# Four mixing layers on one image, the scan layer: TensorE's products grouped by array form, the state contribution moved behind y by channel into its own columns

## The reference, cut to what matters

```python
dA_cs = jnp.cumsum(dA, axis=2)                                   # within the chunk
Lmat = jnp.exp(dA_cs[:, :, :, None, :] - dA_cs[:, :, None, :, :])
att = einsum('bcihn,bcjhn->bcijh', Ch, Bh) * Lmat * dtc          # causal part only
y_intra = einsum('bcijh,bcjhp->bcihp', att, xc)
states = einsum('bcjhn,bcjh,bcjhp->bchpn', Bh, decay_to_end * dtc, xc)
new = carry * dec + st                                           # from chunk to chunk
y_inter = einsum('bcihn,bcih,bchpn->bcihp', Ch, exp(dA_cs), prev_states)
y = y_intra + y_inter + D * x                                    # then LayerNorm over 384, * norm_w + norm_b
out = (y * z) @ out_proj_w.T                                     # z from the input by a projection
```

## Time and profile before

| | before |
|---|---|
| median of three runs | 2561.39 us |
| the profiled execution | 2555.05 us, span of its instructions 2553.0 us |
| mean granted TensorE clock | 0.956 |
| TensorE products, weight loads | busy 2232.7 us (87%), 1652.4 us (65%) |
| VectorE, ScalarE, GpSimd | busy 1667.8, 1305.3, 1113.0 us |
| the scan's steady turns | from about 949 to 1877 us of the span |

### The profile page before, as it was taken

The page is one execution under the profiler, slowest core; times in us unless marked ns, Lnnn a source line. Parts: engine busy times, 40 slices in busy tenths (PEclk is TensorE's granted clock), DMA queues, the critical chain, the costliest instruction groups (busy, mean ns, idle before and its releaser), DMA issues. The chain is left out here.

```text
span 2553.0 us, 63276 instructions
## 1 busy us (share of the span) xinstructions
PE 2232.7 (87%) x22485; PEld 1652.4 (65%) x22612; DVE 1667.8 (65%) x3120; ACT 1305.3 (51%) x2719; POOL 1113.0 (44%) x1393
## 2 busy tenths in 40 slices
PE   0699997998999169999999999999968999789998
PEld 0575645786788047777777777777756656366563
DVE  5345585674575168888888888888863455734557
ACT  0245540084057147777777777777733454334543
POOL 0333150000000147878787878778743222432225
PEclk9999997999999579999999999999989999989999
DMA  8623395415523312222222222222235045950349
GB/s 207 176 78 69 85 330 155 119 31 208 171 41 122 112 42 60 59 59 59 58 60 56 61 56 62 55 61 57 59 87 157 2 89 153 310 165 15 79 123 317
DMA packets 305576, 272.33 MB, mean 107 GB/s; under 512 B 175534, under 2 KB 238798, under 8 KB 299162
## 3 DMA queue, kind: packets, MB, share of 16 engines
q1 hardware_dynamic: 294650, 256.15, 36.1%
q0 software_dynamic: 9280, 6.44, 2.1%
q10 hardware_dynamic: 1496, 7.63, 0.8%
HBM read 165.44 MB, written 81.46 MB: 97 GB/s over the span
## 5 line engine op out<-in xcount | busy, mean ns | idle before, releaser
L1664 DVE TENSOR_TENSOR l_scan_att<-l_scan_decay,l_scan_causal_scores 128x512 f32<-128x512 f32 x384 | 327.4, 853 | 64.2 <-ACT l_scan_decay L1633 64.0
L714 ACT COPY l_arena<-l_body_bank 128x384 f32<-128x384 f32 x192 | 141.3, 897 | 308.3 <-PE l_body_bank L591 308.3
L1627 ACT ACTIVATE l_scan_decay<-l_scan_cum 128x512 f32<-128x512 f32 x384 | 216.3, 597 | 34.4 <-PE l_scan_cum L1519 34.3
L1633 ACT ACTIVATE l_scan_decay<-l_scan_decay 128x512 f32<-128x512 f32 x384 | 227.8, 631 | 4.1
L810 DVE TENSOR_TENSOR l_freq<-l_body_bank,l_filter 128x512 f32<-128x512 f32 x144 | 99.6, 692 | 183.8 <-PE l_body_bank L604 183.8
L1644 ACT ACTIVATE l_scan_yw<-l_scan_y_by_channel,l_scan_norm_b,l_scan_norm_w 128x128 f32<-128x128 f32 x384 | 148.0, 456 | 127.8 <-PE l_scan_y_by_channel L1581 126.8
L1566 PE MATMUL l_scan_gate_projected<-l_scan_xr,l_wf 97*128 97x128 f32 (+1 forms) x1536 | 206.6, 284 | 1.3 <-DVE l_scan_xo L1719 1.2
L1597 PE MATMUL l_scan_gate_projected<-l_scan_yz,l_scan_wo 128*96 128x128 f32 x1536 | 198.5, 279 | 1.1 <-DVE l_scan_yz L1696 1.1
L1597 PEld LDWEIGHTS l_scan_gate_projected<-l_scan_yz,l_scan_wo 128*96 128x96 f32 x1536 | 170.9, 163 | 40.0 <-issue 29.6
L571 POOL TENSOR_TENSOR l_arena<-l_arena 96x512 f32<-96x512 f32 x96 | 122.7, 1278 | 167.2 <-ACT l_arena L779 162.5
L1484 POOL TENSOR_TENSOR l_scan_inter<-l_scan_inter,l_scan_xd 128x384 f32<-128x384 f32 x128 | 128.0, 1000 | 152.5 <-DVE l_scan_inter L1679 152.5
(11 more groups left out here) (193 smaller groups left out, 4995.4 us busy)
## 6 DMA issues: line engine op xcount, KB each, us to landing
l_scan_xc<-convolved_rows SPq DMA_DIRECT2D x128, 224.0 KB, 2.8
x_after<-l_arena SPq DMA_DIRECT2D x64, 384.0 KB, 4.8
l_arena<-x_after SPq DMA_DIRECT2D x64, 384.0 KB, 5.6
convolved_rows<-l_slots SPq DMA_DIRECT2D x48, 441.0 KB
l_conv_x_main<-x_after SPq DMA_DIRECT2D x64, 256.0 KB, 2.6
l_arena<-x_after SPq DMA_DIRECT2D x16, 1024.0 KB, 8.3
prepare_xt<-x SPq DMA_DIRECT2D x8, 1536.0 KB
l_arena<-x SPq DMA_DIRECT2D x32, 384.0 KB, 5.7
```

The costliest lines, as they stand in the source:

```text
L714: nc.scalar.copy(tA[:, b, :, j:j + 2].rearrange("p c q -> p q c"), bank[n % 4][:, 0:2 * C].rearrange("p (q c) -> p q c", q=2)).then_inc(t_ ...
L1627: nc.scalar.activation(decay[:, b % 2, 4 * g:4 * g + 4, :], cum[(b + g) % 2][:], ACT.Relu, scale=-1.0)\
L1633: nc.scalar.activation(group, group, ACT.Exp, scale=-1.0).then_inc(exp_done, 1)
L1664: nc.vector.tensor_tensor(att[:, b, 4 * g:4 * g + 4, :], decay[:, b % 2, 4 * g:4 * g + 4, :], causal[:, b % 2:b % 2 + 1, :].broadcast_to([ ...
```

## The change

On TensorE the transpose of B and C moves to the head of the turn; y by channel follows, then, behind the wait for the state, the state contribution, then the state product; the scores come right behind it, and cumulative 0 and 1 behind them. The contribution is written to the other half of the bank's columns (`half_s`), and no longer waits for the scaling. ScalarE copies B and C before it copies y by channel. VectorE adds the new state right behind att0 instead of behind att1. No operation is added or taken away, and no transfer.

```diff
--- before.py
+++ after.py
@@ -1374,7 +1374,7 @@
         p_bcg = ph.ps("bcg", [128, 2, W])
         p_y = ph.ps("y_intra", [128, D_INNER])
         p_i = ph.ps("y_inter", [128, 2, BANK])
-        half_i = slice(0, D_INNER // 2)
+        half_i, half_s = slice(0, D_INNER // 2), slice(D_INNER // 2, D_INNER)
         p_zo = ph.ps("gate_projected", [128, BANK])
         p_z = p_zo[:, 0:3 * W].rearrange("p (m w) -> p m w", w=W)
         p_o = p_zo[0:CH, 0:2 * W].rearrange("p (k w) -> p k w", w=W)
@@ -1523,6 +1523,11 @@
                 def turn(at):
                     row0, row2, row3, row4 = (at(lag) for lag in (0, 2, 3, 4))
 
+                    if row0:
+                        r, b, n = row0
+                        pe.wait_ge(xc_landed[b], n * 32 + 32)
+                        pe.wait_ge(masked, r + 1)
+                        nc.tensor.transpose(p_bcg[:, 0, :], xc[:, b, CONV_DIM + N_STATE - 128:], ident[:]).then_inc(bc_turned, 1)
                     if row2:
                         r, b, n = row2
                         pe.wait_ge(xs_ready, 3 * r + 3)
@@ -1536,25 +1541,22 @@
                                 last = nc.tensor.matmul(p_yt[h * HEAD:(h + 1) * HEAD, g, :], xdt[:, b % 2, head],
                                                         att[:, b, 4 * g + h, :], start=(g == 0), stop=(g == 2))
                         last.then_inc(yi_done, 1)
-                    if row0:
-                        r, b, n = row0
-                        pe.wait_ge(xc_landed[b], n * 32 + 32)
-                        pe.wait_ge(masked, r + 1)
-                        nc.tensor.transpose(p_bcg[:, 0, :], xc[:, b, CONV_DIM + N_STATE - 128:], ident[:]).then_inc(bc_turned, 1)
-                    if row2:
-                        r, b, n = row2
                         pe.wait_ge(state_ready, r + 1)
+                        for g in range(2):
+                            last = nc.tensor.matmul(p_i[g * N_STATE:(g + 1) * N_STATE, 0, half_s], xc[:, b, D_INNER:D_INNER + N_STATE],
+                                                    xw[:, b % 2, g * D_INNER // 2:(g + 1) * D_INNER // 2], start=True, stop=True)
+                        last.then_inc(st_done, 1)
                         for g in range(2):
                             at = slice(g * N_STATE, (g + 1) * N_STATE)
                             last = nc.tensor.matmul(p_i[:, g, half_i], bct[at, b, 1, :], state[at, :], start=True, stop=True)
                         last.then_inc(inter_done, 1)
                     if row0:
-                        cumulative(row0, 0)
-                        cumulative(row0, 1)
                         r, b, n = row0
                         pe.wait_ge(bc_copied, r + 1)
                         nc.tensor.matmul(p_bcg[:, 1, :], bct[0:N_STATE, b, 0, :], bct[0:N_STATE, b, 1, :], start=True, stop=True)\
                             .then_inc(scores, 1)
+                        cumulative(row0, 0)
+                        cumulative(row0, 1)
                     if row4:
                         r, b, n = row4
                         pe.wait_ge(xr_landed[b], n * 16 + 16)
@@ -1582,13 +1584,6 @@
                         last.then_inc(turned, 1)
                     if row0:
                         cumulative(row0, 2)
-                    if row2:
-                        r, b, n = row2
-                        pe.wait_ge(scaled, r + 1)
-                        for g in range(2):
-                            last = nc.tensor.matmul(p_i[g * N_STATE:(g + 1) * N_STATE, 0, half_i], xc[:, b, D_INNER:D_INNER + N_STATE],
-                                                    xw[:, b % 2, g * D_INNER // 2:(g + 1) * D_INNER // 2], start=True, stop=True)
-                        last.then_inc(st_done, 1)
                     if row4:
                         r, b, n = row4
                         pe.wait_ge(yz_done, r + 2)
@@ -1607,6 +1602,13 @@
 
                 def turn(at):
                     row0, row2, row3 = (at(lag) for lag in (0, 2, 3))
+                    if row0:
+                        r, b, n = row0
+                        act.wait_ge(bc_turned, r + 1)
+                        if not (isinstance(r, int) and r < U):
+                            act.wait_ge(inter_done, r - 2)
+                        nc.scalar.copy(bct[0:N_STATE, b, 0, :], p_bcg[N_STATE:2 * N_STATE, 0, :])
+                        nc.scalar.copy(bct[:, b, 1, :], p_bcg[2 * N_STATE:4 * N_STATE, 0, :]).then_inc(bc_copied, 1)
                     if row2:
                         r, b, n = row2
                         act.wait_ge(yi_done, r + 2)
@@ -1614,11 +1616,6 @@
                         nc.scalar.copy(yt[:], p_yt[:]).then_inc(yt_kept, 1)
                     if row0:
                         r, b, n = row0
-                        act.wait_ge(bc_turned, r + 1)
-                        if not (isinstance(r, int) and r < U):
-                            act.wait_ge(inter_done, r - 2)
-                        nc.scalar.copy(bct[0:N_STATE, b, 0, :], p_bcg[N_STATE:2 * N_STATE, 0, :])
-                        nc.scalar.copy(bct[:, b, 1, :], p_bcg[2 * N_STATE:4 * N_STATE, 0, :]).then_inc(bc_copied, 1)
                         act.wait_ge(att_done, 3 * r)
 
                         def gaps(g):
@@ -1688,6 +1685,11 @@
                         if not (isinstance(r, int) and r < U):
                             dve.wait_ge(yi_done, r - 2)
                         attention(r, b, 0)
+                    if row2:
+                        r, b, n = row2
+                        dve.wait_ge(st_done, r + 2)
+                        dve.wait_ge(faded_done, r + 1)
+                        nc.vector.tensor_tensor(state[:], p_i[0:2 * N_STATE, 0, half_s], faded[:], ALU.add).then_inc(state_ready, 1)
                     if row4:
                         r, b, n = row4
                         dve.wait_ge(yw_done, 3 * r + 3)
@@ -1705,11 +1707,6 @@
                         nc.vector.bn_aggr(mv[:, b], st6[:, b]).then_inc(agg, 1)
                     if row0:
                         attention(row0[0], row0[1], 1)
-                    if row2:
-                        r, b, n = row2
-                        dve.wait_ge(st_done, r + 2)
-                        dve.wait_ge(faded_done, r + 1)
-                        nc.vector.tensor_tensor(state[:], p_i[0:2 * N_STATE, 0, half_i], faded[:], ALU.add).then_inc(state_ready, 1)
                     if row0:
                         attention(row0[0], row0[1], 2)
                     if row4:
```

## The result

The changed kernel is a little slower: 2569.62 us against 2558.57, medians of 20 runs each, ratio **1.0045** with a 95% interval of 1.0032 to 1.0058. The forecast was 2561 on a median of 2561.39, that is no change, with 0.38 on slower. The new median lies inside the forecast's range of 2520 to 2592, but the comparison moved clear of its noise where none was forecast.

The account below looks back on a forecast made before the run. TensorE was taken to bound the scan at 7.54 us a turn, then the path through att0 and yz at 7.555: +2 us in 122 steady turns, -2.5 in first and last, net 0, so 2561 us; range 2520 to 2592.

Parts of the forecast that it names:

- the eight changes: TensorE's array-form changes in a turn: 0.16 us each, three instead of eight, 0.80 off, own work 6.74 us.
- The wait at the output product: TensorE, ready 3.30 us after group 0, waits every turn for yz, which allows the product at 3.08 + att0's length.
- Att0's hold: GpSimd's xdt starts 0.23 us ahead of attention product att0, stretching it to 1.14 in three turns of four; turn 7.66.
- State ahead of yz: VectorE's state update, now between att0 and yz, adds 0.19 us to that path; bounds 0 and 0.34.
- the 0.54 of the rows: Trace-measured time by which a held att0 ends after the GpSimd operation running at its start: 0.54 to 0.55 us.
- the VectorE and GpSimd loop: Scaling to scaling through skip add, xdt, att0, yz and later steps: 7.67 us, hidden before; 0.34 extra per four-turn pass.
- Edits at no price: Side effects taken as free: score waits, B/C copies (0.5 us if cover went), row load, separate columns, earlier state update.
- A: Rival: TensorE stays the bound, its own work 6.74 us a turn, -98 us, 2464; chance 0.06.
- B: Rival: att0 starts ahead of xdt in all turns, unheld, turn 7.2 us, -41 us, 2520; chance 0.20.
- C: Rival: att0 is held in the first turn of a pass too, mean turn 7.755, +26 us, 2588; chance 0.22.
- D: Rival: the new wait costs more, through late GpSimd or load or a lower TensorE clock, 0.3 us a turn, 2598; chance 0.07.
- a case of +0.02 a turn: Main case for the steady scan: mean turn 7.555 against 7.54 us, whole kernel 2561, alone 2551 to 2571; chance 0.45.

Follow-up runs that it names:

- the control with the finer waits: Changed kernel with y by channel waiting for xdt alone and the state contribution for xw, nothing else changed: turn 7.575 us, ratio 1.0042 to the kernel before.

## Why the prediction was wrong

**What bounds before; the eight changes.** Right, as far as the runs show it. In the turn shown, group 0 to group 0 takes 7.59 us, of which 0.79 is the wait for yz; that leaves an estimated 6.80 for TensorE's own work where 6.74 was forecast, and 0.15 for each of the five changes. TensorE's busy time in the stretch fell by 51 us (903.5 to 852.4), less than the 98 forecast for the work, but a busy PE counts a product's passage and not its pace.

**The wait at the output product.** Right in its parts. Output product to group 0: forecast 3.44, measured 3.43. Group 0 to att0: 2.29 and 2.29. State ahead of yz: forecast 0.19, measured 1511.35 - 1510.07 - 1.09 = 0.19. The wait: 3.08 + 1.14 - 3.30 = 0.92 forecast, 0.79 to 0.86 in three turns of the pass and 0.43 in the one with the short att0.

**Att0's hold.** Right in kind and in size for three turns: 1.14 forecast, 1.16, 1.17 and 1.09 measured; turn 7.66 to 7.67 forecast, 7.62 to 7.67 measured. Scaling came 0.32 behind group 0 in the turn shown, forecast 0.38; xdt's lead 0.29, forecast 0.23. The Trainium skill's rule ("SBUF — State Buffer", "Who interferes with whom"), that whoever starts first keeps the port and the other is blocked, is what the pair of turns with a lead of 0.02 us shows, in both directions. Its full block would give 1.50 where xdt leads by nothing, by the rows' 0.83 and 0.67; the trace has 1.36, so for the length the 0.54 of the rows held.

**The step that failed** is the sum: "7.555 - 7.54 = +0.02 us in some 122 steady turns: +2", and "The first turns, at the lower clock, and the last four gain between 0 and 5 x 0.16 in some six turns; I take the middle, -2.5". The waits and the path behind it were right; two terms of it were mis-sized, both by amounts that a forecast of no change could not bear.

(1) The steady turn is 7.576 against 7.535, +0.041, twice what I had: +5.0 us in 122 turns. I had rounded the old turn up to 7.54. In the first turn of a pass I had 7.21 where it measured 7.35, which alone adds 0.035 to the mean of four; the other three gave 0.015 back. In that first turn xdt is the one that is stretched (1.28), xd ends only 0.2 us ahead of y by channel's load, and the control with the finer waits brings that turn to 7.23. But the next turn then takes 7.73, and the mean stays. As I read it, over a pass the VectorE and GpSimd loop sets the time, and I had taken its catching up as bigger than it is.

(2) The first turns cost about 3 us where I had them gain. There TensorE's scores wait for ScalarE's copies of B and C (0.97 and 2.58 us) with the cumulative groups behind them: 10.15 us to the first y by channel against 6.94, and 7.05 with the scores back. In "Edits at no price" I had priced a copy that loses its cover at 0.5 us and taken the cover as given; in the first two turns there is none. The last turns cost 0.4.

Together this makes 5.0 + 3.2 + 0.4 = 8.6 us of scan, beside 8.7 (4.3 to 13.0) in the repeated comparison and 11.5 (8.2 to 14.8) in the first, both from their ratios. The 3 us between the scan and the first comparison are open.

**The rivals.** A falls: the wait is there. B and C were the two sides of an edge, and neither came: three turns stayed held, and the first turn of a pass kept att0 at 0.73. D: the clock stayed at 1.00 in the steady turns. I gave slower 0.38 and same 0.27, and named no change with a case of +0.02 a turn whose own width was 0.08. That no change was the forecast came of two small terms, +2 and -2.5, that happened to cancel; the sign of each should have been argued by itself. The case's width of 0.08 us a turn would have held a change of either sign, so that 2569.62 lies inside it (2551 to 2571) says little for the sum.

## What to carry to other kernels

Before moving work to save it on the bounding engine, walk the chain of the other engines from the first thing that moves later to the last thing that waits for it: here the path through group 0, att0 and yz had 0.5 us of slack (yz's end at 1504.72, the output product's weights at 1505.21). Taking 1.18 us of TensorE's work out of that stretch used the slack up, and 0.54 us of products ahead of group 0 and 0.19 of a state update ahead of yz then stood on the path that set the turn; that was enough to give back all that five saved form changes brought. Look at the first turns by themselves, too: what covers a wait in the steady turns may not be there yet. Where VectorE's product of two SBUF tensors lies on the path that sets the time and meets a GpSimd operation, make the order certain with a semaphore: it gained 1.2% here (0.9919 against 1.0042), and only in the order of TensorE that waited for yz. And an edit that helps in one order of the work can be worth nothing in the other (1.0015 on the kernel before), so try it in both.

## What was not expected of the hardware

The turn of the steady stretch repeats to 0.002 us (7.576 and 7.574) between two executions of the changed kernel that differ by 18 us as a whole (2570.85 and 2552.77). 14.2 of these 18 us lie ahead of the scan, where TensorE's granted clock is at half in other places from run to run, 138.1 us of it in the one and 124.2 in the other. For a change in one stage the turn in the trace tells hundredths of a microsecond where 20 timed runs tell 0.13%.

A lead of 0.02 us in the recorded starts decides which of att0 and xdt is stretched, and by 0.5 to 0.7 us. After a GpSimd operation TensorE's load started 0.2 us later (xd's end to y by channel), after one of VectorE's 0.05.
